# Pauses in VectorE's pair sums, W1's low parts in halves, and a later start of the h1 loads, in a recommender kernel

## The reference

```python
cont_emb = emb_table[:13][None, :, :] * conts[:, :, None]
cate_emb = emb_table[cates]                      # (2048, 26, 64)
cc = concatenate([cont_emb, cate_emb], axis=1)   # (2048, 39, 64)
gram = einsum('bfd,bgd->bfg', cc, cc)
pairs = gram[:, ROWS, COLS]                      # 741 pairs f < g
X = concatenate([cont_emb.reshape(B, -1), cate_emb.reshape(B, -1), pairs], axis=1)
X = relu(layernorm(X @ W1 + b1, ln1_g, ln1_b))   # 1024 columns
X = relu(layernorm(X @ W2 + b2, ln2_g, ln2_b))   # 1024 columns
logit = sigmoid(X @ Wout + bout)
```

## Time and profile before

| | |
|---|---|
| median of 3 runs | 770.68 us (769.99 to 771.81) |
| profiled execution | 770.79 us |
| its span, first to last instruction | 769.3 us |
| mean granted TensorE clock | 0.989 of full speed |
| TensorE matmuls busy | 727.8 us (95%) |
| VectorE busy | 582.9 us (76%) |
| ScalarE busy | 515.9 us (67%) |
| GpSimd busy | 474.0 us (62%) |

### The profile page before, as it was taken

One profiled execution on the slowest core, in us unless ns is written; L12 is line 12 of the kernel. 1 busy time (PEld: TensorE's weight loads), 2 busy tenths in 40 slices (PEclk: granted clock), 3 DMA queues, 4 the chain that ended last, 5 costly groups with the idle time before them and its releaser, 6 DMA issues.

```text
span 769.3 us, 11972 instructions
## 1 busy us (share of the span) xinstructions
PE 727.8 (95%) x3583; PEld 593.4 (77%) x3583; DVE 582.9 (76%) x1735; ACT 515.9 (67%) x977; POOL 474.0 (62%) x450
## 2 busy tenths in 40 slices
PE   5888899999999999999999999999999999999995
PEld 1556678888888878778887787878878888888884
DVE  7577988887888878778787787878786556566568
ACT  4687886877868768686776768768675545535541
POOL 5777777777777777777777777777000443433431
PEclk9999999999999999999999999999999999999998
DMA  8960112111111111111111011113462101101000
GB/s 318 366 236 25 28 52 55 28 54 35 45 54 26 52 26 53 53 26 53 27 53 53 26 53 26 53 27 105 168 223 80 55 29 55 55 27 55 27 1 0
DMA packets 26645, 53.51 MB, mean 70 GB/s; under 512 B 10964, under 2 KB 11272, under 8 KB 26555
## 3 DMA queue, kind: packets, MB, share of 16 engines
q1 hardware_dynamic: 10570, 31.29, 11.7%
q0 software_dynamic: 13312, 13.20, 6.7%
q10 hardware_dynamic: 2736, 8.71, 2.9%
HBM read 45.20 MB, written 11.63 MB: 74 GB/s over the span
## 4 chain that ended last, share of the span: by engine, by line
PE 47%; POOL 27%; issue 15%; DVE 6%; DMA 2%; ACT 2%; POOLq 0%; SPq 0%; ACTq 0%; DVEq 0%
POOL xb L523 26%; PE acc L553 14%; PE acc L554 13%; PE acc L555 13%; PE gr L619 1%; PE tr L619 1%; PE gr L721 1%; PE tr L721 1%; DMA xb<-in_L_rec_emb_table,idx_all 1%; PE tr L577 1%; ACT g_move L807 1%; DMA h_scratch<-h_row 1%; DVE w_lo L1138 1%; DVE g_still L1130 1%; DVE dots L1204 1%
## 5 line engine op out<-in xcount | busy, mean ns | idle before, releaser
L523 POOL DMA_INDIRECT xb<-table_scratch,idx_all x396 | 384.8, 972 | 120.7 <-issue 120.1
L553 PE MATMUL acc<-w_hi,x_hl 128*128 128x512 f32 x416 | 171.6, 412 | 5.7 <-DVE x_hl L1122 5.6
L555 PE MATMUL acc<-w_hi,x_hl 128*128 128x512 f32 x416 | 164.4, 395 | 0.0
L554 PE MATMUL acc<-w_lo,x_hl 128*128 128x512 f32 x416 | 164.0, 394 | 0.0
L537 POOL TENSOR_TENSOR raw_lo<-raw_lo,raw_hi 128x1024 f32<-128x1024 f32 x14 | 33.5, 2391 | 146.4 <-ACT raw_lo L1004 146.4
L553 PE MATMUL acc<-w_hi 128*128 128x512 f32 x256 | 100.9, 394 | 0.0
L555 PE MATMUL acc<-w_hi,w_lo 128*128 128x512 f32 x256 | 99.7, 389 | 0.0
L801 ACT CAST g_still<-x_hl 64x384 fp32r<-64x384 f32 (+1 forms) x128 | 98.0, 766 | 2.5
L554 PE MATMUL acc<-w_lo,w_hi 128*128 128x512 f32 x256 | 99.7, 389 | 0.0
L553 PEld LDWEIGHTS acc<-w_hi,x_hl 128*128 128x128 f32 x416 | 79.5, 191 | 20.9 <-issue 4.5
L555 PEld LDWEIGHTS acc<-w_hi,x_hl 128*128 128x128 f32 x416 | 79.1, 190 | 18.2
(11 more groups left out here) (121 smaller groups left out, 1300.1 us busy)
## 6 DMA issues: line engine op xcount, KB each, us to landing
raw_lo<-in_L_rec_W SPq DMA_DIRECT2D x26, 512.0 KB, 5.5
h_scratch<-h_row ACTq DMA_DIRECT2D x16, 512.0 KB, 2.9
raw_hi<-h_scratch SPq DMA_DIRECT2D x16, 512.0 KB, 3.3
xb<-table_scratch,idx_all POOLq DMA_INDIRECT x396, 2.4
table_scratch<-in_L_rec_emb_table SPq DMA_DIRECT2D x4, 781.2 KB, 7.2
raw_hi<-in_L_rec_W SPq DMA_DIRECT2D x6, 512.0 KB, 5.8
raw_hi<-in_L_rec_b SPq DMA_DIRECT2D x1, 512.0 KB, 3.9
raw_hi<-in_L_rec_ln_g SPq DMA_DIRECT2D x1, 512.0 KB, 4.9
```

Of the source, the lines that this page charges most:

```text
L523: done = nc.gpsimd.indirect_dma_start(out=to, out_offset=None, in_=table, in_offset=at_row)
L553: nc.tensor.matmul(o, a, w, start=first, stop=False)
L554: nc.tensor.matmul(o, a, v, start=False, stop=False)
L555: return nc.tensor.matmul(o, b, w, start=False, stop=last)
```

## The change

Three edits. In `cate_pairs`, ahead of the additions 4, 8, 13 and 18, VectorE waits for the addition in front, and a semaphore increment of its own stands behind the wait. In `w1_lo_part`, each of the 19 subtractions of 1024 columns becomes two of 512, and the second waits for the first. On SyncE, the first two loads of h1 also wait until the last group of gathers of the last tile has landed; everything behind them in SyncE's program waits with them.

```diff
+PAIR_BREAKS = (4, 8, 13, 18)
...
+        w1_half = sem("w1_half")
...
+        pair_parts = sem("pair_parts")
...
             sp.wait_ge(w1_free, 4)
             sp.wait_ge(h1_out, 16 * 2)
+            a, b = GROUPS[NG - 1]
+            sp.wait_ge(gathered[NG - 1], 16 * 2 * (b - a) * TILES)
             load_h1(sp, 0, 0)
             load_h1(sp, 1, 1)
...
                 dve.wait_ge(w1_rounded, k + 1)
                 if k >= 1:
                     dve.wait_ge(w1_split, k)
-                TT(w1_lo[:, k, :], raw_lo[k][:, :], w1_hi[:, k, :].bitcast(F32),
-                   ALU.subtract).then_inc(w1_split, 1)
+                for h, signal in enumerate((w1_half, w1_split)):
+                    part = slice(h * HALF, (h + 1) * HALF)
+                    TT(w1_lo[:, k, part], raw_lo[k][:, part], w1_hi[:, k, part].bitcast(F32),
+                       ALU.subtract).then_inc(signal, 1)
+                    if h == 0:
+                        dve.wait_ge(w1_half, k + 1)
...
                 for f in range(CATE - 1):
+                    if f in PAIR_BREAKS:
+                        last.then_inc(pair_parts, 1)
+                        dve.wait_ge(pair_parts, len(PAIR_BREAKS) * x + PAIR_BREAKS.index(f) + 1)
+                        stands_alone(dve)
                     last = TT(chosen[:, cate_at(f):cate_at(f + 1)], S[:, f, f + 1:CATE], S[:, f + 1:CATE, f], ALU.add)
                 last.then_inc(chosen_done, 1)
```

## The result

The changed kernel takes 775.36 us (median of 6 executions, 772.56 to 778.06), the kernel before 770.89 (769.82 to 774.99) beside it: ratio 1.0051, 95% interval 1.0028 to 1.0074. It is slower by half a per cent, and outside the predicted range of 766.0 to 773.0. The profiled execution is its slowest: 778.06 us, span 776.5, so what follows shows more of the loss than a typical execution has. The two executions with a mean granted clock of 0.988 (the kernel before has 0.989 in its profile) took 772.56 and 773.84 us; the four with 0.985 or less took 774.37 to 778.06.

The account below looks back on a forecast made before the run. TensorE and GpSimd were taken to bound the kernel in turns, GpSimd in late tiles. Gather relief -9.75, start +2.6, tiles +6.1 and end +0.6 us made -0.45, so 770.3 us, range 766.0 to 773.0.

Parts of the forecast that it names:

- What bounds the kernel: Tiles: TensorE and GpSimd take turns, GpSimd bounding the late tiles; relieving GpSimd can give at most 9.75 us.
- the two paces: Time per tile: 31.98 us over the first four periods, TensorE's need; 33.06 us over the nine behind them.
- the long gather beside the sums: GpSimd: a gather started within VectorE's pair sums took 1.47 us, some 0.5 us of GpSimd's period.
- The pause: VectorE's pair sums: 0.24 us for each of four waits, stretching the run from 2.41 to 3.37 us.
- my lower bound: Pair sums: waits with no increment behind them would still lengthen the run by 0.61 us.
- The second rival: Pair sums: a longer wait makes the kernel slower, 773 us at 0.22 us per wait; chance 0.20.
- The first rival: Pair sums: waits stay under the 0.42 us of cover and GpSimd alone keeps pace, 764.3 us; chance 0.16.
- The price per tile: TensorE waiting for the second group's low part: 0.47 us per tile, 6.1 us over 13 tiles (2.5 to 7.7).
- the cover: Second group's low part: VectorE can be 0.42 us later before TensorE's k-tile 4 has to wait.
- The start: Before the statistics of tile 1: W1's halves and the first runs of sums make it 2.6 us late (2.1 to 2.9).
- A fall of the granted clock in more stretches than now: Clock: would make the kernel slower than the sum says; no size or chance given.
- The end and SyncE: Last tile's sums cost 0.6 us (0.3 to 0.8); holding h1 loads costs nothing, gives the last gather at most 1.1 us.

Follow-up runs that it names:

- pauses alone: Kernel before plus the four waits in the sums with increments; W1's parts whole, no added SyncE wait: 771.50 us beside 771.72, ratio 0.9998.
- bare waits, timed: Kernel after without the increments behind its four waits, W1's parts whole, SyncE's wait kept: 765.68 us beside 770.79 of the kernel before, ratio 0.9942.
- bare waits, one execution: Kernel after without the increments behind its four waits, W1's parts whole, SyncE's wait kept, run once: 766.85 us beside 770.97 of the kernel before.
- halves alone: Kernel before plus W1's low parts in halves; no waits in the sums, no added SyncE wait: 771.80 us, ratio 1.0000.
- after, with bare waits: Kernel after without the increments behind its four waits, W1's halves and SyncE's wait kept: 767.87 us beside 773.72 of the kernel before, ratio 0.9921.

## Why the prediction was wrong

It is told by its own steps.

**What bounds the kernel: right.** The limit of -9.75 us, the two paces and the long gather beside the sums are all borne out: with bare waits the tiles run at 32.08 to 32.15 us and the landing waits are gone.

**The pause: right in size.** I said 3.37 us for the run; it is 3.36 to 3.48 in all tiles but one (3.75), and the idle time at a pause is the 0.15 to 0.16 us that I took. With an increment behind it a pause takes 0.24, 0.23, 0.22 and 0.23 us more than a plain step between sums. A bare wait takes 0.10 to 0.12 more: the run is 2.92, 0.44 longer, where my lower bound for such waits was 0.61. The bound took the 0.10 us that lie between W1's parts; between sums a bare wait leaves some 0.03 us idle. And I had taken bare waits for a bound, not for a version to build. The second rival's mechanism (a longer pause) is not what made the kernel slower. (One of its sums is off: at 0.22 us its own 3.0 us for each 0.05 give 773.9, not 773.) The first rival's 764.3 us is near what bare waits give, 765.68, but it was for another kernel, so that is no merit of it.

**The price per tile: a size too small.** I took 0.47 us per tile, 6.1 in all. TensorE's period is 32.64 against its own 31.98: 0.66, 8.5 in all. Of it 0.57 is explained: the run is some 0.97 us longer than before and the cover, read over all steady tiles, is 0.40 rather than 0.42. Of the last 0.09, about 0.04 is two periods of 32.92 and 32.82 us against a median of 32.60; the rest has not been put down to a row, and bare waits leave 0.06 as well (0.44 longer, 0.40 covered, 0.10 lost). This alone makes the kernel 2.4 us slower than forecast. With the pauses alone the 13 tiles come to -1.85 where I had -3.65.

**The start: the step that failed.** The prediction says "The start is late by 2.6 us in all (2.1 to 2.9)"; it is 8.17. The priced terms that can be read were good: four parts in halves take 5.98 us for 5.21, 0.77 for 0.76, and TensorE's wait for the low part at the end of them grew by just that, 2.53 to 3.30 us. What was not priced, and makes up most of the rest, is a lower clock of TensorE, above all behind that wait. The windows' rows for 20:32, 52:62 and 100:112 (the granted clock is the third number from the end), before, after, and of the pauses alone:

```profile
20.00:32.00 12.00, 9.41 (x32) 6.32 (x31) 7.32 (x20) 6.23 (x9) 9.56 (x9) 0.86 0.89 320
52.00:62.00 10.00, 8.07 (x50) 7.25 (x49) 6.53 (x15) 7.45 (x16) 7.56 (x9) 0.90 0.10 27
100.00:112.00 12.00, 11.55 (x56) 9.05 (x55) 11.10 (x44) 10.03 (x17) 9.26 (x10) 0.96 0.10 26
```

```profile
20.00:32.00 12.00, 8.56 (x24) 5.87 (x23) 8.78 (x23) 6.40 (x9) 9.26 (x10) 0.72 0.89 322
52.00:62.00 10.00, 8.16 (x32) 7.29 (x33) 5.95 (x12) 5.63 (x11) 7.80 (x8) 0.66 0.10 26
100.00:112.00 12.00, 9.40 (x38) 7.91 (x38) 9.64 (x27) 7.93 (x14) 9.21 (x10) 0.72 0.24 72
```

```profile
20.00:32.00 12.00, 9.49 (x33) 6.30 (x31) 7.38 (x20) 6.25 (x9) 9.56 (x9) 0.86 0.90 320
52.00:62.00 10.00, 8.05 (x50) 7.24 (x49) 6.49 (x15) 7.41 (x16) 7.56 (x9) 0.90 0.11 28
100.00:112.00 12.00, 10.60 (x48) 8.22 (x48) 11.04 (x44) 10.18 (x17) 9.23 (x10) 0.96 0.12 29
```

The pauses leave the clock as it was; with the halves, TensorE is busy for 8.16 of 10 us after that wait and gets 32 matmuls through in place of 50. The timelines inside it, before and then after: eight of the dot products' matmuls take 1.80 us for 1.03, and the product's matmuls 0.63 us each for 0.39, 0.43 from start to start in place of 0.23. TensorE is at 1.2 GHz there, the lower of its two levels.

```profile
52.89 1.03 PE L619 MATMUL gr<-g_move,g_still 128*128 128x124 f32 x8
...
55.60 0.39 PE L554 MATMUL acc<-w_lo,x_hl 128*128 128x512 f32 x1
55.83 0.39 PE L555 MATMUL acc<-w_hi,x_hl 128*128 128x512 f32 x1
```

```profile
54.37 0.40 PE L560 MATMUL acc<-w_hi,x_hl 128*128 128x512 f32 x1
...
55.37 1.80 PE L624 MATMUL gr<-g_move,g_still 128*128 128x124 f32 x8
...
60.06 0.63 PE L558 MATMUL acc<-w_hi,x_hl 128*128 128x512 f32 x1
60.49 0.63 PE L559 MATMUL acc<-w_lo,x_hl 128*128 128x512 f32 x1
```

What the fall costs shows in the seven profiles with tiles of 32 us. "Stretch" is the time from the matmul behind that wait (51.44 before) to the one that waits for the dot copies (97.14 before), in us:

| kernel | W1's parts | the wait | clock 52:62 | stretch | statistics 1 |
|---|---|---|---|---|---|
| before | whole | 2.53 | 0.90 | 45.70 | 121.15 |
| pauses alone | whole | 2.54 | 0.90 | 45.79 | 122.07 |
| bare waits, timed | whole | 2.53 | 0.94 | 45.78 | 122.40 |
| bare waits, one execution | whole | 2.34 | 0.66 | 48.63 | 125.27 |
| halves alone | halves | 3.30 | 0.66 | 50.53 | 127.26 |
| after, with bare waits | halves | 3.30 | 0.66 | 49.11 | 127.50 |
| after | halves | 3.30 | 0.66 | 49.65 | 129.32 |

The two profiles of bare waits are of one and the same program: the fall alone costs it 2.9 us. It came in three of three profiles with halves and in one of four with whole parts, at the shortest wait of all. So it looks likelier with the halves, which seven profiles can't prove; they aren't its only cause, and the length of that wait alone doesn't decide it. Of the 5.6 us that the start is later than I said, some 3.1 lie in this stretch (3.95 less the 0.84 of VectorE's time priced there, which no run tells apart), 1.6 ahead of it, and 1.0 behind it, where the clock of 100:112 is 0.72 for 0.96. Ahead of it the clock of 20:32 is 0.72 too, but the timed bare waits had 0.72 there and came only 0.8 us late to that matmul, so about 0.8 us is put down to nothing. The prediction had named this ("A fall of the granted clock in more stretches than now") and given it no price and no chance.

**The end and SyncE: near enough.** The last tile costs +0.31 us against 0.6 (0.3 to 0.8). Layer 2 keeps its 190.5 us behind statistics 15, with SyncE's wait and without, so it costs nothing at that end. Whether it gives the last gathers anything wasn't told apart: with the pauses TensorE doesn't wait for them in the last tile, with SyncE's wait or without.

**Sum.** Start +8.17 for +2.6, tiles -1.21 for -3.65, last tile +0.31 for +0.6: +7.27 for -0.45, 5.6 of the 7.7 us between them in the start. That is the slowest execution; the median is 2.7 us below it, and by the executions' granted clocks it is probably the start that costs less there. The interplay is the point. The gathers' lead worked like a buffer: with the halves alone, a start 6.11 us late left 2.41 at tile 14. The pauses leave TensorE no faster than the gathers in any tile, so a late start stays late. By the statistics, the pauses alone come to -0.6, the halves alone to +3.4, both with SyncE's wait to +7.3 us; by the medians, 0, 0 and 0.5%. In the profile of the halves alone, at 774.2 us, the kernel was at the upper end of its executions (770.83 to 774.20), so its +3.4 overstates the typical one.

**The rule on a semaphore between operations.** The Trainium skill ("VectorE: DVE Perf Modes", section "The DRAIN you can't avoid") says that a semaphore after each of a chain of copies costs nothing extra over one after the last. These runs don't bear it out for a wait between sums of 25 and fewer elements: each bare wait costs 0.10 to 0.12 us, and 0.23 with the increment behind it. No run here had long operations in a chain to test the rule where it is stated.

## What to carry to other kernels

When two engines take turns as the bound, work out what slack each has, and what that slack absorbs: an edit that is free alone can be dear with another that uses the same slack. Here the small waits that let gathers in paid (ratio 0.9942 and 0.9921), and the same waits with one further instruction behind each cost all of it and more (1.0051). For an edit that lengthens a wait of TensorE in the start, price the possible fall of its clock as a case of its own.

## What the runs showed that was not expected

- A bare wait every four or five short sums is enough for the gathers to pass beside them: 0.94 to 0.99 us each for those that start within the sums, and a mean of 961 and 952 ns over all 396, with no landing wait left. A single pause with its increment did nearly as well (26 of 28).
- With bare waits the gathers' lead still shrinks by some 0.4 to 0.6 us a tile; 16 tiles are too few for it to run out.
- The same program had looped tiles of some 44 us in some sets of executions and 32 in others, on one chip even, with layer 2 unchanged (190.5 us behind statistics 15 in both). What sets it stays open.
- The clock of the start differs between executions of one kernel: bare waits with whole parts had 0.66 in the stretch 52:62 in one profile and 0.94 in the other.
